# A mixture-of-experts kernel on one core: in-place split of the weight tails, the first weight piece split early, routing shares computed late, the weight wait moved ahead of the down products

## The reference

```
H   = x @ W.T + scaling * (x @ A[idx].T) @ B[idx].T      # conditioning
p   = softmax_integer(H @ w_gate.T); top 2 per token, renormalised
out = x + sum_e combine[:, e] * ((silu(H @ w1[e].T) * (H @ w3[e].T)) @ w2[e].T)
```

## Time and profile before

| | us |
|---|---|
| median of 3 runs | 231.97 (231.13 to 232.19) |
| the profiled execution | 231.47 |
| its span in the trace | 229.4 |
| PE busy | 205.3 (89%) |
| POOL busy | 150.7 (66%) |
| DVE busy | 100.7 (44%) |
| ACT busy | 85.5 (37%) |

### The profile page before, as it was taken

How to read it: one execution, slowest core, us unless ns; L and a number is a source line. 1 busy time by engine, 2 the same in 40 slices (tenths; PEclk the granted TensorE clock), 3 DMA queues, 4 the chain that set the end, 5 groups by cost and what they waited for, 6 DMA issues and landing times.

```text
span 229.4 us, 3961 instructions
## 1 busy us (share of the span) xinstructions
PE 205.3 (89%) x1227; PEld 176.8 (77%) x1227; DVE 100.7 (44%) x297; ACT 85.5 (37%) x232; POOL 150.7 (66%) x131
## 2 busy tenths in 40 slices
PE   7699995999999999999993799099999999999993
PEld 5479973888888888888982688088887988888891
DVE  0758886353343534344332135013533444336814
ACT  2656760599423333232331123012322323226610
POOL 8100066969969998998999799989984453188000
PEclk9999998899999999999999799859999999999999
DMA  6994317999345104064505540440051111019004
GB/s 158 414 372 160 123 60 223 379 372 331 118 161 176 37 24 139 24 206 130 171 18 188 181 139 16 169 140 23 1 186 69 70 49 69 23 47 322 22 3 183
DMA packets 16146, 32.66 MB, mean 142 GB/s; under 512 B 2080, under 2 KB 10400, under 8 KB 16000
## 3 DMA queue, kind: packets, MB, share of 16 engines
q1 hardware_dynamic: 12304, 25.17, 33.0%
q0 software_dynamic: 2160, 5.64, 7.0%
q10 hardware_dynamic: 1664, 1.61, 2.2%
HBM read 25.59 MB, written 6.82 MB: 141 GB/s over the span
## 4 chain that ended last, share of the span: by engine, by line
POOL 37%; PE 32%; DMA 14%; issue 10%; ACT 3%; POOLq 1%; DVE 1%; SPq 0%; DVEq 0%; ACTq 0%
POOL w_all L423 18%; PE gu L1095 9%; DMA rows<-cond_rows,src_i 8%; POOL rows L417 7%; POOL w_all L490 6%; PE gu L1102 4%; DMA expert_rows<-rows,dst_i 3%; DMA x<-x_t 3%; PE gu L981 3%; PE ya L1132 2%; POOL w_all L436 2%; POOL expert_rows L448 2%; PE ht L1109 2%; PE ya L1133 2%; PE ya L1134 2%
## 5 line engine op out<-in xcount | busy, mean ns | idle before, releaser
L1095 PE MATMUL gu<-w_all,xs_hi 128*128 (+2 forms) x276 | 75.2, 396 | 13.5 <-POOL w_all L436 11.8
L1095 PEld LDWEIGHTS gu<-w_all,xs_hi 128*128 128x128 f32 x276 | 48.6, 195 | 22.2 <-issue 17.5
L835 DVE TENSOR_TENSOR hid<-gu,sg 128x256 f32<-128x256 f32 x46 | 19.5, 425 | 91.9 <-ACT sg L593 88.8
L593 ACT ACTIVATE sg<-gu 128x256 f32<-128x256 f32 x46 | 17.7, 385 | 93.9 <-PE gu L1102 91.8
L423 POOL TENSOR_TENSOR w_all<-raw,w_all 128x1024 fp32r<-128x1024 f32 (+2 forms) x15 | 46.8, 3123 | 1.1
L1102 PE MATMUL gu<-w_all,xs_lo 128*128 (+1 forms) x138 | 42.1, 387 | 2.6 <-DVE xs_lo L827 2.6
L417 POOL DMA_INDIRECT rows<-cond_rows,src_i x23 | 23.1, 1005 | 30.0 <-DMA cond_rows<-c_rows 23.7
L1132 PE MATMUL ya<-w_all,h_hi 128*128 (+1 forms) x115 | 38.7, 337 | 0.0
L448 POOL DMA_INDIRECT expert_rows<-rows,dst_i x20 | 19.7, 987 | 21.1 <-DVE hid L835 8.7
L1133 PE MATMUL ya<-w_all,h_hi 128*128 (+1 forms) x115 | 32.9, 286 | 0.0
L1134 PE MATMUL ya<-w_all,h_lo 128*128 (+1 forms) x115 | 32.5, 282 | 0.0
(11 more groups left out here) (193 smaller groups left out, 280.1 us busy)
## 6 DMA issues: line engine op xcount, KB each, us to landing
raw<-expert_weights SPq DMA_DIRECT2D x6, 896.0 KB, 4.8
raw<-expert_weights SPq DMA_DIRECT2D x6, 640.0 KB
raw<-expert_weights SPq DMA_DIRECT2D x6, 512.0 KB
expert_rows<-zeros SPq DMA_DIRECT2D x1, 2048.0 KB
rows<-expert_rows SPq DMA_DIRECT2D x8, 256.0 KB, 4.7
cond_rows<-c_rows ACTq DMA_DIRECT2D x4, 256.0 KB, 2.1
raw<-x_t SPq DMA_DIRECT2D x1, 1024.0 KB
out_t<-raw SPq DMA_DIRECT2D x4, 256.0 KB, 2.2
```

The lines of the kernel that those rows point to most:

```text
L1095: nc.tensor.matmul(out, stay_hi[:, kc * P:(kc + 1) * P], moving(at, part + first + kc * P, n), start=kc == 0 and part == HI_COLS, stop=False)
```

## The change

- The tail is copied once, together with piece 2 (`HI_PIECES`: 1536 columns instead of 1280), to all 128 partitions of its place; the lower half is then overwritten in place by its low part. `tail_hi`, and the waits ahead of `tail_low`, are gone, and `raw`'s piece 2 is given back by `w_ready` itself.
- GpSimd splits experts 4 to 7 in another order: the high copy of piece k+1 goes ahead of the subtraction of piece k. `SCATTERED` shifts one scatter from behind expert 5's split to expert 7's.
- ScalarE copies expert 0's first piece early (ahead of `g_both`), VectorE subtracts it in two halves (`first_lo`) between its early steps. ScalarE's copies for experts 2 and 3 start one item later.
- The routing shares (`weights_of_choices`) leave VectorE's part ahead of the items and are computed in four parts at items 54 to 57 (`SHARES_AT`); ScalarE stores them at item 58, and GpSimd reads them behind scatter 15 (`SHARES_BEHIND`), not ahead of the last 13 scatters.
- TensorE waits for the weights of the next slot in the last item of a slot, ahead of that item's down products.

```diff
+HI_PIECES = [PIECES[0], PIECES[1], slice(DOWN_AT, HI_COLS)]
-SCATTERED = {4: (0, 2), 5: (2, 5), 6: (5, 6), 7: (6, 7)}
+SCATTERED = {4: (0, 2), 5: (2, 4), 6: (4, 5), 7: (5, 7)}
+SHARES_AT = ITEMS - 15
+SHARES_BEHIND = 15
...
                     if turn_of(e) and k < 2:
                         sp.wait_ge(raw_free[k], turn_of(e))
+                    elif turn_of(e):
+                        sp.wait_ge(w_ready, in_raw_before(e) + 1)
...
             def tail_low(e):
-                recent = gathered_beside(e - 1, 2) if e > 1 else range(*GATHERED[0])
-                for s in [*recent, *gathered_beside(e, 0), *gathered_beside(e, 1)]:
-                    pool.wait_ge(rows_in[s], 16)
-                if e in SCATTERED:
-                    pool.wait_ge(scattered, 16 * (SCATTERED[e][0] + min(2, SCATTERED[e][1] - SCATTERED[e][0])))
-                return nc.gpsimd.tensor_tensor(stack_part(e, 1), raw_tail(e, LOWER), as_f32(tail_hi[e % 2][LOWER, :]),
-                                               ALU.subtract)
+                stack = stack_part(e, LOW_HALF)
+                return nc.gpsimd.tensor_tensor(stack, raw_tail(e, LOW_HALF), as_f32(stack), ALU.subtract)
...
-                steps += 2
-                nc.gpsimd.tensor_copy(tail_hi[e % 2][:, :], raw_tail(e)).then_inc(whi_step, 1)
-                nc.gpsimd.tensor_copy(stack_part(e, 0), raw_tail(e, slice(0, TAIL))).then_inc(whi_step, 1)
-                pool.wait_ge(whi_step, steps)
                 tail_low(e).then_inc(w_ready, 1)
-                pool.wait_ge(w_ready, e + 1)
-                pool.sem_inc(raw_free[2], 1)
                 beside_piece(e, 2)
...
             for s in range(SCATTERED[EXPERTS - 1][1], SENT):
                 pool.wait_ge(hid_done, s + PACE)
                 scatter(s)
+                if s == SHARES_BEHIND:
+                    pool.wait_ge(share_at_ready, 1)
+                    pool.wait_ge(share_out, 16)
+                    for l in range(DIRECT):
+                        nc.gpsimd.indirect_dma_start(
...
+            def first_lo(half):
+                cols = slice(half * ITEM_COLS, (half + 1) * ITEM_COLS)
+                dve.wait_ge(whi_ready, 1)
+                return nc.vector.tensor_tensor(lo_part(0, cols), raw[:, cols], as_f32(hi_part(0, cols)), ALU.subtract)
...
-                    if j == 0 and s:
-                        pe.wait_ge(w_ready, code)
...
                 if 1 <= i <= ITEMS:
                     turn_hidden(i - 1)
+                if j == 2 and s + 1 < SLOTS:
+
+                    pe.wait_ge(w_ready, at_of[s + 1][0])
```

More of the change, by code:

```diff
@@ L166, in moe_kernel @@
         h_lo = [sb(f"h_lo{i}", [P, 2 * P], F32R) for i in range(HBUFS)]
-        tail_hi = [sb(f"tail_hi{i}", [P, DIM], F32R) for i in range(2)]
+        raw_low_tail = sb("raw_low_tail", [P, DIM])
         raw = sb("raw", [P, HI_COLS])
@@ L259, in moe_kernel @@
         raw_low_in = [sem(f"raw_low_in{k}") for k in range(len(PIECES))]
-        raw_free = [sem(f"raw_free{k}") for k in range(len(PIECES))]
-        w_split0 = sem("w_split0")
+        raw_free = [sem(f"raw_free{k}") for k in range(len(PIECES) - 1)]
         w_ready = sem("w_ready")
@@ L306, in lo_part, with stack_part @@
             return w_all[:, ring_at(e) + HI_COLS + cols.start:ring_at(e) + HI_COLS + cols.stop]
[L308 to L310 removed]
+        def stack_part(e, part):
+            return w_all[part, ring_at(e) + STACK_AT:ring_at(e) + STACK_AT + DIM]
         def from_raw(e):
@@ L367, in _ @@
                 raw_weights(e)
-            for k in range(len(PIECES)):
-                sp.wait_ge(raw_free[k], EXPERTS - 2)
+            sp.wait_ge(w_ready, EXPERTS)
             sp.dma_start(x_back, x_dram[:, :, :]).then_inc(x_back_in, 16)
@@ L579, in _ @@
             expert_hi(0, 2)
-            expert_tail_hi(0)
+            expert_hi(1, 0)
             c_copy(2)
             c_copy(3)
-            for k in range(len(PIECES)):
-                expert_hi(1, k)
-            expert_tail_hi(1)
+            expert_hi(1, 1)
+            expert_hi(1, 2)
             def silu(i):
@@ L890, in _, with weights_of_choices @@
-            for k in range(2):
-                expert_lo(0, k).then_inc(w_split0, 1)
-                dve.wait_ge(w_split0, k + 1)
-                dve.sem_inc(raw_free[k], 1)
+            def weights_of_choices(part):
+                by_choice = weight[:, :].rearrange("p (k t) -> p k t", t=TILES)
+                if part == 0:
+                    chain(nc.vector.tensor_scalar(rs[:, total, :], rs[:, total, :], 1.0, None, ALU.max))
+                    beside(nc.vector.reciprocal(rs[:, most, :], rs[:, total, :]))
+                    chain(nc.vector.tensor_tensor(masked[:, :, :], mask[:, :, :],
+                                                  full(poly).unsqueeze(1).broadcast_to([P, TOP, TILES * EXPERTS]),
+                                                  ALU.mult))
+                if part == 1:
+                    chain(nc.vector.tensor_reduce(weight[:, :],
+                                                  masked[:, :, :].rearrange("p k (t e) -> p (k t) e", e=EXPERTS),
+                                                  AX_X, ALU.add))
+                    chain(nc.vector.tensor_tensor(by_choice, by_choice,
+                                                  rs[:, most, :].unsqueeze(1).broadcast_to([P, TOP, TILES]),
+                                                  ALU.mult))
+                if part == 2:
+                    chain(nc.vector.tensor_tensor(weight_sum[:, :], weight[:, 0:TILES], weight[:, TILES:], ALU.add))
+                    chain(nc.vector.reciprocal(rs[:, total, :], weight_sum[:, :]))
+                if part == 3:
+                    nc.vector.tensor_tensor(by_choice, by_choice,
+                                            rs[:, total, :].unsqueeze(1).broadcast_to([P, TOP, TILES]),
+                                            ALU.mult).then_inc(weight_ready, 1)
```

129 lines of the change are left out of this document (51 added, 78 removed).

## The result

The changed kernel takes 219.41 us (median of 4, 219.05 to 220.21), the kernel before 231.69 us beside it (231.13 to 232.19): ratio 0.9475, 95% interval 0.9438 to 0.9513. The profiled execution is the one of 220.21 us (span 218.1), the longest of the four.

A forecast was written before the change was run, and what follows sets the result against it. GpSimd's weight splits were taken to bound the kernel until slot 16, TensorE after. Terms of -10.4, -0.2 and +1.1 us gave -9.5 on 231.47, 222.0 (222.5 against the median); 222.2 us was stated, range 218.8 to 225.6.

The forecast's parts named there:

- GpSimd leads until slot 16, and savings ahead of it move the end: GpSimd's splits set the pace to the last split; slot 16 was to start 10.4 us earlier.
- Start, 1.5 us: GpSimd begins expert 1 1.5 us earlier, because VectorE finishes expert 0 sooner.
- I take 0.2: Deduction of 0.2 us from the start's 1.7, for gathers running beside expert 0's last big VectorE subtraction.
- Landing waits, 3.4 us: GpSimd's `tail_low` no longer waits for gathers to land: 3.4 us saved in two waits.
- Between two experts, 2.1 us: GpSimd's next instruction follows `tail_low` sooner, with the wait and increment gone: 2.1 us saved.
- Inside experts 4 to 7, 0.95 us each: GpSimd's single tail copy and reordered copies save 0.95 us an expert, 3.8 us for four.
- Loads as the rival: Rival: piece 2's copy, asked for earlier, waits for its load; 226.0 us at most, or slower than before; chance 0.06.
- TensorE's waits, 1.5, 4 and 1 us, and the clock behind the last: TensorE's three waits for GpSimd's splits; rival, chance 0.10: low clock behind the last, 223.9 to 224.8 us.
- The wait ahead of the down products, 0.2 us: TensorE's moved weight wait gains 0.03 us a slot, 0.2 us over the six slots that count.
- the stall moves rather than goes: Claim that TensorE's 0.27 us idle at each slot start mostly stays, at the wait's new place.
- stall gone: Rival: TensorE's slot-start stall vanishes, 1.6 us gained instead of 0.2, and shares hidden: 219.5 us; chance 0.08.
- The late shares, 1.1 us: Shares stored late delay the last scatters and read-back, making TensorE 1.1 us late in item 68.

The follow-up runs named there:

- e4: Changed kernel with the waits for recent gathers' landing put back ahead of the tail's subtraction (`tail_low`): 224.74 us, ratio 0.9702 to the kernel before.
- e3: Changed kernel with GpSimd's old order for experts 4 to 7, each copy directly ahead of its own subtraction: 220.62 us, ratio 0.9528 to the kernel before.
- e7: Changed kernel with the second input of VectorE's two long expert 0 subtractions from PSUM, not SBUF (two low parts left out): 221.36 us.
- e6: Changed kernel with shares computed, stored and read early as before, and all 20 scatters behind expert 7's split: 223.36 us, ratio 0.9616 to the kernel before.
- e8: Changed kernel with expert 0's first piece split where it stood before, not early: 224.78 us, ratio 0.967 to the kernel before.
- e1: Changed kernel with TensorE's wait for the weights back at the slot's start, behind the down products: 221.16 us, ratio 0.9552 to the kernel before.
- e2: Kernel before with only TensorE's wait for the next slot's weights moved ahead of the last item's down products: 230.03 us, ratio 0.9933.
- e10: Changed kernel with scatters 7 to 11 held until item 53 is done, so scatters 7 to 15 follow without a pause: 229.64 us, ratio 0.9878.
- e11: Changed kernel with early shares, all 20 scatters behind expert 7's split and spaced, one share read behind scatter 18, two behind 19: 213.75 us.
- e5: Changed kernel with the shares worked out early (items 15 to 18) and read ahead of the last scatters, as before: 220.03 us, ratio 0.9487.

## Why the prediction was right, and where it was off

222.2 us was predicted with 218.8 to 225.6; it is 219.4, inside that range and outside the forecast's own of 220.3 to 223.8. Against the profiled execution before, the difference is -11.3 us where -9.5 was summed (the median's is -12.3; this execution lost 0.75 us to the low clock early). By its steps:

- *GpSimd leads until slot 16, and savings ahead of it move the end.* Right: e4's last split is 5.0 us later and its time 5.3, e3's 1.6 and 1.2. It holds for losses; of savings, e7's 1.9 us and e6's 9.0 were lost again behind the last split.
- *Start, 1.5 us.* Mis-sized: 0.3 us, taken from the first gather. The term "I take 0.2" for gathers beside the split was 1.4 (1.21 + 0.94, less the 0.23 and 0.54 that the first two gathers of before, 1.18 and 1.49 us, took over 0.95). The row that decided it was misread: the gather of 1.49 us was not 0.54 us longer beside a whole subtraction, but beside the last 0.66 us of one, so it had stood for most of what was left. The rule of the Trainium skill (SBUF — State Buffer, Who interferes with whom) was set aside on this row. By it the start was to gain 0.2 us, nearly what was measured, and e7 shows that it bears, though the same page infers that a subtraction of this kind wouldn't hold up a DMA. The early split is still worth its place: e8's last split ends 1.3 us later.
- *Landing waits, 3.4 us.* Right.
- *Between two experts, 2.1 us.* Larger: the gap ahead of expert 7's first copy, 0.96 us before, is gone, where 0.1 was taken. From expert 1's start to the last split's end 10.7 us were saved where 9.6 were summed. This made up for most of what the start lacked, and that the split's end came within 1 us of the forecast is in part luck.
- *Inside experts 4 to 7, 0.95 us each.* Right (expert 4 takes 20.37 us for 21.31).
- *Loads as the rival.* Not seen: no copy waited for `raw` here, and only one, 0.61 us, in e6, where they ask earlier.
- *TensorE's waits, 1.5, 4 and 1 us, and the clock behind the last.* They were 4.51, 3.45 and 2.67 us: with shorter slots TensorE came to them earlier than thought. Full clock followed the last.
- *The wait ahead of the down products, 0.2 us.* The step that was most wrong: "the stall moves rather than goes". It goes, 0.30 us for each slot, 1.8 us over the last six; e1 and e2 show it from both sides. The rival "stall gone" had a chance of 0.08 and 219.5 us, and it describes what happened better than the forecast with 0.62.
- *The late shares, 1.1 us.* Mis-sized: from slot 22's start to the end 20.08 us by the profile against 19.78 before, and in e1 and e3, which keep the late shares, 19.75 and 19.80. Last scatter 34.9 us behind slot 16's start, not 38.3: the store was issued 25.0 us behind that start (181.76), where 26.4 was worked out from longer slots, and the first read (183.94) followed it by 2.2 us, where a landing of 4.2 was assumed.

So the part on GpSimd was right in mechanism, with two wrong sizes that nearly cancel. The 1.8 us by which the forecast is too slow come from TensorE's part: 1.6 us for the stall that was thought to move and 1.1 for the shares, less 0.9 us at the last split's end, most of it the low clock early in this execution.

## What to carry to other kernels

A wait whose value is worked out in registers belongs ahead of the last products of a block, not where the next block starts: moving it there, with two of its register operations, took a stall of 0.3 us away at every slot start. Before work is taken off the engine that leads, look at what it will then issue in a row: here 9 us freed on GpSimd were lost until the scatters were spaced, and with them spaced the kernel takes 213.75 us. A short VectorE instruction with two SBUF inputs is no longer short beside GpSimd's long ones, so look at what will run beside it. A change of the order on one engine is timed over several executions, since such stalls come in some and not in others.

## What the runs showed of the hardware

- Indirect DMAs that follow each other on GpSimd every 1.28 us can hold back TensorE's semaphore increments: 4 us for three of them in e10, 3.7 us in e6, up to 2.5 us behind five in a row in the kernel before. They needn't: behind the row of seven in the changed kernel none was late. At one each 2.3 us (the change) none was over 0.4 us late.
- A gather that starts beside a VectorE subtraction with both inputs in SBUF stands until that one ends: 2.16 and 1.89 us in the changed kernel, 2.97 in e8, against 0.95 alone, and 1.18 and 0.95 in e7 with one input in PSUM. One that started 0.11 us ahead of the subtraction took 1.18 us.
- The other way round, a VectorE product of 16 columns with both inputs in SBUF took 4.85 us beside GpSimd's copies and subtraction in e11, and 0.17 us without them.
- The clock fell to 0.50 behind waits of 4.51 us and, in e10, 3.14 us, and stayed at 1.00 behind waits of 3.45 and 2.67 us in the changed kernel. The length of the last wait alone doesn't decide it: it also fell behind one of 2.60 us in e10 (138.7 to 142.1) and one of 1.74 us in e5 (86.5 to 89.9).
